# A four-layer megakernel on one core: the attention outputs and the lag chain in another order, and another interleaving of the four-bit MLP

## What is computed

```python
x = x + tanh(g_xattn[0]) * L0_xattn(layernorm(x), ctx, ctx, ...)   # softmax attention, 16 heads, rope
x = x + tanh(g_ffn[0])   * L0_ffn(layernorm(x), ...)               # 2 of 8 experts for each sequence
x = x + tanh(g_xattn[1]) * L1_xattn(layernorm(x), ctx, ctx, ...)   # autocorrelation attention
x = x + tanh(g_ffn[1])   * L1_ffn(layernorm(x), w_gate, w_up, w_down)
```

```python
def fp4_quant_dequant(x):             # blocks of 16 along the last axis
    scale = maximum(max(abs(xb)) / 6, 1e-12)
    q = _GRID[searchsorted(_MID, abs(xb / scale))] * sign(xb) * scale
def fp4_linear(x, w):
    return einsum('bsk,nk->bsn', fp4_quant_dequant(x), fp4_quant_dequant(w))
h = silu(fp4_linear(x, w_gate)) * fp4_linear(x, w_up)              # width 352
return fp4_linear(h, w_down)
```

## Time and profile before

| | us |
|---|---|
| median of three runs | 293.07 |
| the profiled execution, its time | 291.37 |
| its span, first to last instruction | 289.2 |
| PE busy | 257.1 (89%) |
| DVE busy | 199.6 (69%) |
| ACT busy | 162.0 (56%) |
| POOL busy | 119.2 (41%) |
| mean granted TensorE clock | 0.976 |

### The profile page before, as it was taken

How to read it: one execution, slowest core, us unless ns; L and a number is a source line. 1 busy time by engine, 2 the same in 40 slices (tenths; PEclk the granted TensorE clock), 3 DMA queues, 4 the chain that set the end, 5 groups by cost and what they waited for, 6 DMA issues and landing times.

```text
span 289.2 us, 6270 instructions
## 1 busy us (share of the span) xinstructions
PE 257.1 (89%) x2176; PEld 200.9 (69%) x2176; DVE 199.6 (69%) x538; ACT 162.0 (56%) x370; POOL 119.2 (41%) x170
## 2 busy tenths in 40 slices
PE   7999999999899999999999998898856779767955
PEld 5655466666578779999999985556734547544855
DVE  3997678889987762522222249768758799998981
ACT  2479976666686666766666666636351724343421
POOL 4564599996202132199822105303533031313120
PEclk9999999999999999999999999999997969997999
DMA  7998000000000278776777500000000000000001
GB/s 194 376 356 345 4 3 0 2 2 2 0 3 2 82 316 341 291 297 279 303 295 295 221 0 3 0 1 2 0 0 0 2 1 0 18 18 20 19 19 57
DMA packets 12159, 30.15 MB, mean 104 GB/s; under 512 B 992, under 2 KB 5216, under 8 KB 12000
## 3 DMA queue, kind: packets, MB, share of 16 engines
q1 hardware_dynamic: 12128, 29.75, 27.3%
HBM read 9.75 MB, written 1.05 MB: 37 GB/s over the span
## 4 chain that ended last, share of the span: by engine, by line
PE 64%; DVE 16%; ACT 8%; issue 6%; DMA 3%; POOL 2%; SPq 1%; DVEq 0%; POOLq 0%
PE ps L1316 11%; PE ps L1305 11%; PE ps L1161 6%; PE ps L1494 4%; PE ps L1135 4%; DVE s_region L281 4%; PE ps L1148 4%; PE ps L1063 3%; PE ps L1436 2%; PE ps L1054 2%; PE ps L1171 2%; PE ps L1055 2%; PE ps L1353 2%; DVE s_region L1000 2%; DVE s_small L1010 2%
## 5 line engine op out<-in xcount | busy, mean ns | idle before, releaser
L575 ACT ACTIVATE s_region<-ps,s_region 128x128 f32<-128x128 f32 x144 | 41.1, 369 | 22.0 <-PE ps L1305 21.7
L871 DVE SCALAR_TENSOR_TENSOR s_ctxT<-ps,s_region,s_ctxT 128x64 f32 x72 | 18.1, 282 | 44.2 <-PE ps L1316 44.2
L1305 PE MATMUL ps<-s_region 128*128 128x128 f32 x288 | 38.5, 276 | 0.3
L1316 PE MATMUL ps<-s_region 128*128 128x128 f32 x288 | 38.0, 275 | 0.0
L288 POOL TENSOR_TENSOR s_region<-s_region,s_small 128x704 f32<-128x704 f32 (+2 forms) x13 | 17.4, 1341 | 47.3 <-DVE s_region L281 47.3
L1305 PEld LDWEIGHTS ps<-s_region 128*128 128x128 f32 x288 | 35.0, 192 | 1.0 <-DMA s_region<-s_wall 0.6
L1316 PEld LDWEIGHTS ps<-s_region 128*128 128x128 f32 x288 | 35.0, 192 | 0.2 <-issue 0.2
L253 POOL TENSOR_TENSOR s_small<-s_small,s_par 128x4 f32<-128x4 f32 (+3 forms) x14 | 15.5, 1106 | 45.2 <-DVE s_small L236 45.2
L400 POOL COPY s_region<-s_xt 128x64 f32 x72 | 14.8, 236 | 32.1 <-PE ps L1305 22.1
L1494 PE MATMUL ps<-s_region 128*128 128x352 f32 x64 | 25.0, 542 | 2.4 <-ACT s_region L652 2.3
L518 ACT COPY s_region<-ps 128x512 f32<-128x512 f32 x32 | 17.2, 593 | 16.2 <-PE ps L1148 16.2
(11 more groups left out here) (216 smaller groups left out, 507.6 us busy)
## 6 DMA issues: line engine op xcount, KB each, us to landing
s_region<-s_wall SPq DMA_DIRECT2D x36, 514.0 KB, 3.1
s_wall<-wall SPq DMA_DIRECT2D x8, 514.0 KB, 8.7
s_par<-par SPq DMA_DIRECT2D x1, 1316.0 KB, 10.9
s_x<-x SPq DMA_DIRECT2D x2, 512.0 KB, 7.2
out<-s_x SPq DMA_DIRECT2D x8, 128.0 KB, 1.8
s_region<-ffn SPq DMA_DIRECT2D x1, 560.0 KB, 3.6
s_ctxT<-ctxT SPq DMA_DIRECT2D x2, 256.0 KB, 4.6
s_ctxT<-ctxT SPq DMA_DIRECT2D x1, 512.0 KB, 7.1
```

What stands on the lines that cost most here:

```text
L575: ins = act.activation(hg[j % 3][:, c, :], ps[:, j % 3, RPT * S * c:RPT * S * (c + 1)], ACT.Gelu, bias=wbuf[j % 6][:, FF + FC * D + c:FF + ...
L871: dve.scalar_tensor_tensor(row, ps[:, 4 + j % 2, S * k:S * k + S], w, row, ALU.mult, ALU.add).then_inc(m["acc_done"], 1)
L1305: ins = mm(ps[:, j % 3, RPT * S * c:RPT * S * (c + 1)], w[:, P * c:P * c + P], xg[j % 4], start=True, stop=True)
L1316: ins = mm(ps[:, 4 + j % 2, 0:RPT * S], w[:, FF + D * c:FF + D * c + D], hg[j % 3][:, c, :], start=(c == 0), stop=(c == FC - 1))
```

## The change

- Lags: in PE's queue the order is `sum_heads(0)`, `turn_sums(0)`, `sum_heads(1)`, `correlate(0)`, `turn_sums(1)`, `correlate(1)`; ACT's copies follow.
- Outputs: `out_product(0)` and `out_tokens(0)` stand between the spectra 4 to 7; on DVE `attention_out(0)` comes ahead of `roll_values(6)` and `(7)`; `out_tokens` writes banks 5, 1, 5, 6, so group 1 no longer waits for the addition of group 0, and group 3 for none. On DVE `attention_out(2)` and its statistics stand ahead of `x_round(0)`. The weights' transposes come later.
- MLP: `x_round(1)` stands ahead of pair 0; `x_scale` and `x_round` of later groups inside pair steps, one step earlier. In a pair step the rounding of the pair before comes last, behind the shrinking of this one. On PE `gate(q + 2)` and `up(q + 1)` are apart, `turn_h(q - 2)` stands directly ahead of `down(q - 2)`, one iteration later than before. ACT's magnitude of a pair comes behind its copy of `hT`.
- The clock matmuls of the last iterations (9 behind `turn_h(5)`, 3 behind `turn_h(6)`, 3 behind `turn_h(7)`) become 5 and 5: five behind `down(5)` and five between `down(6)` and `turn_h(7)`.

```diff
+OUT_BANK = (5, 1, 5, 6)
...
@@ POOL @@
-            for q in range(PAIRS):
+            for q in range(6):
                 values_added(q)
             powers(pool, 0, 4)
+            values_added(6)
+            values_added(7)
             powers(pool, 4, 8)
+            powers(pool, 8, 12)
             x_unscale(0)
-            powers(pool, 8, 12)
             powers(pool, 12, 16)
             x_unscale(1)
             for q in range(1, PAIRS + 1):
                 u = (q - 1) % 2
+                if q in (1, 3):
+                    x_unscale((q + 3) // 2)
...
-                if q in (2, 4):
-                    x_unscale(q // 2 + 1)
@@ ACT @@
             sums_read(0)
+            sums_turned(0)
             sums_read(1)
-            sums_turned(0)
             sums_turned(1)
...
+            weights_turned(0)
             normalise(act, 0, 4, m["xn_d"], 11)
             y1_turned(2)
+            weights_turned(1)
+            y1_turned(3)
             normalise(act, 4, 8, m["xn_d"], 12)
             x_magnitude(0)
-            y1_turned(3)
+            weights_turned(2)
+            normalise(act, 8, 12, m["xn_d"], 13)
             turned_x(0)
-            normalise(act, 8, 12, m["xn_d"], 13)
             silu(0)
             x_magnitude(1)
             normalise(act, 12, 16, m["xn_d"], 14)
-            for q in range(PAIRS + 1):
+            for q in range(PAIRS + 2):
                 if q + 1 < PAIRS:
                     silu(q + 1)
+                if q in (0, 2, 4):
+                    turned_x(q // 2 + 1)
+                if q >= 2:
+                    act.wait_ge(m["ht_done"], q - 1)
+                    act.copy(hT[q % 2].rearrange("p a k b -> p a (k b)"), ps[:, 5:7, 0:MT * P]).then_inc(m["ht_used"], 1)
                 if q < PAIRS:
                     magnitude(q)
-                if q in (1, 3):
-                    x_magnitude((q + 3) // 2)
-                if q >= 1:
-                    act.wait_ge(m["ht_done"], q)
-                    act.copy(hT[(q - 1) % 2].rearrange("p a k b -> p a (k b)"), ps[:, 5:7, 0:MT * P]).then_inc(m["ht_used"], 1)
-                if q in (0, 2, 4):
-                    turned_x(q // 2 + 1)
+                if q in (0, 2):
+                    x_magnitude(q // 2 + 2)
@@ DVE, pair_step @@
-                if second:
-                    dve.wait_ge(m["hm_done"], q)
-                    dd.step(fp4_off(dve, hd[w], hm[w], hh[w].rearrange("p a n -> p (a n)")))
-                    fp4_off(dve, hd[w], hm[w], hd[w]).then_inc(m["hd_done"], 1)
...
                     k = dd.mark(dve.tensor_reduce(hmx[n3], blocks(flat), AX, ALU.max, apply_absolute_value=True))
-                if q >= 3:
-                    finish(q - 3)
-                if first:
+                    if q in (1, 3):
+                        x_round((q + 3) // 2)
+                    if q == 2:
+                        x_scale(3)
+                    if q >= 3:
+                        finish(q - 3)
...
+                    if q == 0:
+                        x_scale(2)
+                else:
+                    finish(q - 3)
+                if q >= 1:
+                    dve.wait_ge(m["hm_done"], q)
+                    if q >= 3:
+                        dve.wait_ge(m["hq_done"], q - 2)
+                    dd.step(fp4_off(dve, hd[w], hm[w], hh[w].rearrange("p a n -> p (a n)")))
+                    fp4_off(dve, hd[w], hm[w], hd[w]).then_inc(m["hd_done"], 1)
@@ DVE @@
             out_and_stats(0)
+            roll_values(6)
+            roll_values(7)
             out_and_stats(1)
             x_scale(0)
+            out_and_stats(2)
             x_round(0)
-            out_and_stats(2)
             out_and_stats(3)
             x_scale(1)
-            for q in range(PAIRS + 3):
+            x_round(1)
+            for q in range(PAIRS + 1):
                 pair_step(q)
-                if q in (0, 2, 4):
-                    x_round(q // 2 + 1)
-                if q in (1, 3):
-                    x_scale((q + 3) // 2)
+            for q in range(PAIRS - 2, PAIRS):
+                finish(q)
@@ PE @@
             turn_x(0)
             keep_clock(2, 7)
-            gate_up(0)
+            gate(0)
+            up(0)
+            gate(1)
             for q in range(PAIRS + 2):
                 if q + 1 < PAIRS:
-                    gate_up(q + 1)
+                    up(q + 1)
                 if q >= 2:
+                    turn_h(q - 2)
                     down(q - 2)
-                if 1 <= q <= PAIRS:
-                    turn_h(q - 1)
+                if q in (0, 1, 3):
+                    turn_x(1 if q == 0 else (q + 3) // 2)
                 if q < 2:
                     keep_clock(4, 7)
-                if PAIRS - 2 <= q <= PAIRS:
-                    keep_clock(9 if q == PAIRS - 2 else 3, 0)
-                if q in (0, 2, 4):
-                    turn_x(q // 2 + 1)
+                if q + 2 < PAIRS:
+                    gate(q + 2)
+                if PAIRS - 1 <= q <= PAIRS:
+                    keep_clock(5, 0)
```

64 lines of the change are left out of this document (32 added, 32 removed).

## The result

The changed kernel takes **289.38 us** (median; 288.58 to 290.27), the kernel before 293.0 in the same comparison: ratio 0.9876, 95% interval 0.9846 to 0.9905, so 3.6 us faster (2.8 to 4.5) where 1.9 were forecast. The time lies in the stated range, but the gain is almost twice the sum.

The account below looks back on a forecast made before the run. Three limits in turn: a chain through engines, DVE in the MLP, then a chain again. Lags +0.2, outputs -0.9, loop -3.3 and tail +2.1 give -1.9 us, from 293.07 to 291.2 us; range 289.0 to 293.2 for 8 in 10.

Parts of the forecast that it names:

- lags: Third layer's lags: between a gain of 0.9 and a loss of one ACT copy, 0.8, taken as +0.2 us.
- outputs (front, without lags): Outputs' stretch: first MLP product at 225.7 against 226.6, so -0.9 us, between -1.9 and +0.3.
- MLP loop: First MLP product to last: -3.3 us from 46.20 to 42.9, between -1.5 and -4.8.
- tail: Last product to last addition, 14.1 us before: +0.8 at full clock, +2.1 in all, bounds 0.8 and 3.9.
- `x_round(0)`, which still ends near 218.3: Outputs: group 0's rounding ends no sooner, since additions 1 and 2 now precede it; the first product's gate and factor need it.
- the stall: MLP loop: DVE's 1.24 us wait before a late product goes, with 0.08 of overlap, a gain of 1.3 us.
- contention: MLP loop: DVE instructions lengthened by meeting POOL's, 2.7 us before; 1.2 counted as gained, bounds 0 and 2.7.
- gates are now issued about a step ahead: MLP loop: behind a product only the factor remains, 1.3 us, or 2.6 at 1.2 GHz, within a 5.4 us step.
- I take 1.3 of it: Tail: TensorE's lower clock on the path costs 3.1 us at most, of which 1.3 was counted.
- Rival 1: Clock stays up before pair 0 and in the tail: -4.0 us, 289.1 us in all; chance 0.15.
- Rival 2: MLP loop: contention with POOL only moves, its 1.2 us not gained: -0.7, 292.4 us; chance 0.11.
- The transposes' rule: Tail: transposes do not count as activity for the clock gate, so 1.2 GHz throughout and the sum 1.8 us higher.

## Why the prediction came out as it did

The direction and the working by stretches held; the size did not. Point by point, as changed part:

| term | forecast | measured |
|---|---|---|
| lags | +0.2 | -0.1 |
| outputs (front, without lags) | -0.9 | -1.4 |
| MLP loop | -3.3 | -3.85 |
| tail | +2.1 | +1.0 |
| sum | -1.9 | -4.3 |

**Lags.** Right that nothing much came of it; the sign was the other one.

**Outputs.** The step that failed is "`x_round(0)`, which still ends near 218.3". Counted from the first addition it ended 1.07 sooner: 219.59 - 174.90 = 44.69, before 218.29 - 172.53 = 45.76. The first addition comes 2.4 us sooner (32.62 from that start for 34.99 before), and I had let additions 1 and 2 in front of the rounding eat all of it. They eat little, because DVE waited there anyway, 1.69 for ACT's magnitude in the earlier trace rows; with addition 2 in the gap 0.32 of that wait is left. What ends last before `x_round(0)` is the magnitude in both kernels, and ACT's queue sets it (timeline, ACT, changed kernel):

```profile
215.49 0.58 ACT L620 COPY s_region<-ps 128x512 f32<-128x512 f32 x1 [1.73 <-PE ps L1455]
215.97 1.65 ACT L245 ACTIVATE s_xn<-s_x,s_small 128x128 f32<-128x128 f32 x4
217.52 0.61 ACT L669 ACTIVATE s_region<-s_region 128x512 f32<-128x512 f32 x1
```

The magnitude starts 42.62 from the first addition, 43.70 before, 1.08 sooner. DVE's input for it was 1.97 sooner; the rest went into the copy `y1_turned(3)`, which now stands in front and waited 1.73 for TensorE. Half of the 1.07 came back as a loss behind the rounding. From the end of `x_round(0)` to the product the chain took 7.9 us (219.59 to 227.51) instead of the 7.4 of the prediction: the gate alone, mostly at 1.2 GHz, took 2.8 (ACT's copy of the input ends at 222.06, its SiLU starts at 224.86) where I had 2.3 with the clock's share. The links behind the rounding were the right ones, and the clock fell as before. The upper bound of this term, +0.3, does not follow from its own numbers, which give -0.3 (224.7 + 1.6 against 226.6).

**MLP loop.** Almost right, and can now be closed: `x_round(1)` gives -1.35, the stall -1.32, a second stall of 0.19 before (239.19) with its overlap -0.27, contention 2.73 before and 0.40 + 0.69 = 1.09 now, -1.64, and the maximum's wait +0.72 (product to maximum 0.91 to 0.99 instead of 0.80 in seven steps, 1.08 together, less 0.36 in three early steps that had such a wait before: 0.12 at the first product and 0.12 each in front of two L1015). Sum -3.86, measured -3.85. Contention was undersized by 0.4, the second stall was not counted. The number for the stall was right and its reason, "gates are now issued about a step ahead", was not: with gate and factor together again the stall did not return.

**Tail.** The +0.8 at full clock was right, piece by piece: the last rounding 2.83 (2.8 forecast), and `turn_h(7)` directly behind the clock matmuls. TensorE of the changed kernel:

```profile
278.61 1.60 PE L1537 MATMUL ps<-s_region 128*128 128x128 f32 x12 [0.89 <-ACT s_region L691]
280.05 1.28 PE L1126 MATMUL ps<-s_par 128*128 128x128 f32 x10
281.17 0.82 PE L1527 MATMUL ps<-s_par,s_region 128*128 128x128 f32 x6
```

POOL had been done at 279.94 (278.55 plus 1.39), so those five cost 1.2. The step that failed is "I take 1.3 of it". The clock cost nothing in three profiles with this tail code (15.14 to 15.15) and 0.5 in three others (15.64 to 15.66). I had taken the idle stretch of the earlier trace rows, 0.71 of 3.00 us busy, as the nearest row; the tail with its clock matmuls had TensorE busy for 9.91 of 15.20 us at a clock of 1.00. The kernel with no clock matmuls there had the clock down for most of the tail, 16.56, so the mechanism is real, and the profile with the five behind `down(5)` alone (14.44) has them keep most of its cost away.

With the front at -1.4 and no clock term in the tail the sum would have been -3.7: these two steps are 1.8 of the 2.4 us that were missing, the loop 0.5. Rival 1, the clock stays up, was half right, in the tail and not in front; that its 289.1 is within 0.3 us of the result is luck, since its front term, 0.8 for a clock that stays up there, did not come about. Rival 2 was wrong: most of the contention is gone, since POOL's 1.4 us now stand beside the product and the maximum, which no row shows lengthened.

The transposes' rule of the Trainium skill ("TensorE: Matmul & The Clock Gate", Part 4: PE-mode transpose) put the tail at 1.2 GHz throughout. The trace of the changed kernel does not show that, with 18 transposes, the 36 rows of three `down` and 20 of clock matmuls in it at a clock of 1.00. In the kernel without clock matmuls the clock was low for most of the tail, but the last `down` took 1.60, full clock, so the whole of the rule's forecast is not seen there either; whether transposes or idle time brought the clock down, no run here separates. The rule of the Trainium skill in "SBUF — State Buffer", Who interferes with whom, fits the meetings that cost time, though not every meeting: see the last section.

## What to carry to other kernels

Where instructions of two engines hold each other up, put the one's long instruction beside those of the other whose rows are never lengthened (here the product with an operand in PSUM and the maximum): that took 1.6 us of waiting out of the loop with no work removed, 0.9 net of what the maximum now waits, and undoing this order alone cost 1.3. When two halves of a change do not add up, split the remainder by part before explaining it: here it was 1.1 us, and half of it was the clock of one execution. Before counting on room that opens on one engine, read what the instruction waits for on the others: `x_round(0)` and `x_round(1)` both waited for ACT. Cut a profile at the first instruction the change can reach, before comparing two spans; here the code ahead of it varied by 2.8 us, and the part behind it repeated within 0.3 us in two profiles each of the two kernels; in the tail the clock still moves it by 0.5.

## What the runs showed of the hardware

- The same code ahead of the change took between 172.06 and 174.90 us in the fourteen profiles, while the MLP loop took 42.35 to 42.37 in the ten of the changed DVE order, in five of which the clock fell in its first 16 us.
- TensorE's clock in one and the same code falls in one execution and not in the next: in the ten profiles in which TensorE's work from the last product to the tail's first `down` is the same, that `down` took 1.60 us four times, 2.39 twice, 2.85 once and 2.93 three times.
- POOL also waits for DVE. Its 128x4 instruction, 0.20 us alone, took 0.63 where DVE's two roundings (218.17 to 219.59) ran; DVE had started first (timeline, POOL, changed kernel):

```profile
214.84 0.20 POOL L256 TENSOR_TENSOR s_small<-s_small 128x4 f32<-128x4 f32 x1
...
219.01 0.63 POOL L256 TENSOR_TENSOR s_small<-s_small 128x4 f32<-128x4 f32 x1
```

It ended at 219.64, 0.05 behind the rounding. The Trainium skill, "SBUF — State Buffer", Who interferes with whom, has the pair of ports go to whichever engine started first, for the whole of its instruction; the trace agrees, and before the change no row had shown this side of it. It does not hold for every pair of instructions: POOL's other 128x4 instruction, a power, ran from 217.93 to 218.94, before and beside the first of the same two roundings, and neither was longer than alone (1.01, and 1.42 for the pair):

```profile
217.93 1.01 POOL L254 TENSOR_TENSOR s_small<-s_small,s_par 128x4 f32<-128x4 f32 x1 [2.89 <-DVE s_small L237]
```
